# Last stage of a four-stage image kernel: planes and pixels fetched from SBUF to SBUF, and the first tile's features made among the channel maxima

## The reference

```
patches = unfold(x, 3x3, stride 2, padding 1)      # (B, C, 3, 3, 128, 128)
x1 = patches.max(axis=1)    # maxima over the 32 channels, 9 rows
x2 = patches.max(axis=2)    # maxima over the rows of a patch, 96 rows
x3 = patches.max(axis=3)    # maxima over the columns of a patch, 96 rows
y  = relu(batchnorm(conv_w @ concat(x1, x2, x3)))  # 32*9*4 rows
out = mean over the 9 taps of patches * y          # 32*2*2 rows, laid back to 256 x 256
```

## Time and profile before

| | |
|---|---|
| runs | 3294.06 us median of 3 (3288.66 to 3294.98) |
| profiled execution | 3293.31 us, span 3291.5 us |
| PE matmul busy | 2702.1 us (82%) |
| DVE busy | 2660.9 us (81%) |
| ACT busy | 1813.8 us (55%) |
| POOL busy | 1831.8 us (56%) |
| DMA moved | 419.22 MB |
| mean granted TensorE clock | 0.935 |

### The profile page before, as it was taken

How to read it: one execution, slowest core, us unless ns; L and a number is a source line. 1 busy time by engine, 2 the same in 40 slices (tenths; PEclk the granted TensorE clock), 3 DMA queues, 4 the chain that set the end, 5 groups by cost and what they waited for, 6 DMA issues and landing times. The chain is left out here.

```text
span 3291.5 us, 45789 instructions
## 1 busy us (share of the span) xinstructions
PE 2702.1 (82%) x12733; PEld 2092.2 (64%) x12733; DVE 2660.9 (81%) x3579; ACT 1813.8 (55%) x2343; POOL 1831.8 (56%) x1296
## 2 busy tenths in 40 slices
PE   0086698899989579799999569889998957979998
PEld 0035577677757458577774468667775745857776
DVE  8985887788885898688888598878888499868887
ACT  7743655566543455565655265566564345555654
POOL 2013173599950436199990317269995044629998
PEclk9998899999999789899999879999999978989999
DMA  6732001988860200688880200289885020068984
GB/s 254 251 91 77 1 0 38 231 220 222 193 174 1 77 1 0 169 222 218 209 228 32 77 0 0 56 230 225 218 192 158 1 77 0 0 183 218 227 208 114
DMA packets 116200, 419.22 MB, mean 127 GB/s; under 512 B 16565, under 2 KB 30693, under 8 KB 105354
## 3 DMA queue, kind: packets, MB, share of 16 engines
q1 hardware_dynamic: 96058, 374.65, 44.1%
q10 hardware_dynamic: 18432, 38.54, 3.3%
q0 software_dynamic: 1616, 4.90, 0.5%
HBM read 340.57 MB, written 75.26 MB: 126 GB/s over the span
## 5 line engine op out<-in xcount | busy, mean ns | idle before, releaser
L895 POOL TENSOR_TENSOR work<-work 128x512 f32<-128x512 f32 x960 | 1283.3, 1342 | 415.4 <-DVE work L1307 314.8
L549 PE MATMUL psum<-workr,w 128*128 128x512 f32 (+1 forms) x5760 | 1366.9, 397 | 67.2 <-ACT workr L765 50.6
L549 PEld LDWEIGHTS psum<-workr,w 128*128 128x128 f32 (+1 forms) x5760 | 1086.5, 189 | 346.9 <-issue 51.4
L1298 DVE SCALAR_TENSOR_TENSOR work<-psum,work 128x512 f32<-128x512 f32 x1152 | 738.1, 679 | 34.9 <-POOL work L895 21.4
L518 PE MATMUL psum<-workr 128*128 128x512 f32 x2304 | 553.7, 403 | 21.5 <-DVE workr L1195 21.5
L869 POOL TENSOR_TENSOR work<-img 128x520 f32 (+1 forms) x256 | 387.2, 1544 | 284.7 <-DVE workr L1167 255.7
L518 PEld LDWEIGHTS psum<-workr 128*128 128x128 f32 x2304 | 441.6, 192 | 135.0 <-issue 24.7
L859 POOL TENSOR_TENSOR work<-work 128x1024 f32<-128x1024 f32 x40 | 114.1, 2886 | 485.2 <-DVE work L1081 483.0
L745 ACT CAST workr<-psum 128x650 fp32r<-128x650 f32 x128 | 90.0, 703 | 419.4 <-DVE psum L1274 411.8
L420 PE MATMUL psum<-work,taps 128*128 x1152 | 261.6, 391 | 44.4 <-DVE work L1039 44.4
L1271 DVE TENSOR_TENSOR psum<-psum,work 128x650 f32<-128x650 f32 x128 | 107.9, 843 | 210.0 <-ACT psum L738 209.7
(11 more groups left out here) (188 smaller groups left out, 3582.6 us busy)
## 6 DMA issues: line engine op xcount, KB each, us to landing
work<-gn_dram SPq DMA_DIRECT2D x256, 585.0 KB, 10.7
work<-gn_dram SPq DMA_DIRECT2D x256, 146.2 KB, 3.8
work<-gn_dram SPq DMA_DIRECT2D x128, 292.5 KB, 4.8
work<-in_x SPq DMA_DIRECT2D x16, 2048.0 KB, 7.2
img<-in_x SPq DMA_DIRECT2D x32, 1024.0 KB, 11.4
work<-in_mixw SPq DMA_DIRECT2D x64, 512.0 KB, 4.9
out_x<-work ACTq DMA_DIRECT2D x120, 256.0 KB, 6.4
gn_dram<-img SPq DMA_DIRECT2D x24, 1040.0 KB, 16.9
```

Of the source, the lines that this page charges most:

```text
L549: mm = T.matmul(bank(m % 6), w5[wt][0:kr, P * n:P * n + P], ft[0:kr], start=(i == 0), stop=(i == 4))
L895: G.tensor_tensor(acc_t[v], acc_t[v], pd_t[(9 * v + n) % 6], ALU.add).then_inc(s_acc, 1)
L1298: V.scalar_tensor_tensor(out=tile4(pd_t[m % 6]), in0=tile4(psum[:, m % 6, :]), scalar=0.0, in1=rv[:, q, y0:y0 + RT, x0:x0 + WO], op0=ALU.m ...
```

## The change

gn_dram and its stores are gone. load_planes and load_pixels read img itself. load_pixels does it with 16 transfers per pair, one for each quadrant and copy, where there were four. The waits on a stored chunk become waits on s_gn3, the normalised chunk. At the end of an image SP waits until all planes and pixels have landed before it goes on to the next image's rows.

The features of tile 0 are moved: ACT makes them (prepare(0)) right after the eight normalisations and before it copies the maxima; DVE's three steps for it stand behind reductions 20, 21 and 24, whose loop is written out. The features of tile 1 (prepare(1)) and the first two restores come after the stores to mx_dram. mxq moves from bank 0 to bank 5, and PE waits for the maxima's copies before the sixth output, which takes that bank.

```diff
+FIRST = (20, 21, 24)
...
-        mxq = psum[:, 0, :].rearrange("p (m2 m1 w) -> p m1 m2 w", m2=2, m1=2)
+        mxq = psum[:, 5, :].rearrange("p (m2 m1 w) -> p m1 m2 w", m2=2, m1=2)
...
-                    sp.dma_start(a_t[k][0:32, :], gn_dram[0:32, n9]).then_inc(s_ab3[k], 16)
+                    sp.dma_start(a_t[k][0:32, :], img[0:32, n9]).then_inc(s_ab3[k], 16)
...
                 def load_pixels(u8, k):
-                    for n in range(4):
-                        sp.dma_start(r_t[k][32 * n:32 * n + 32, :].rearrange("p (q n) -> p q n", q=4),
-                                     byq[:, :, ds(u8 * PW, 9 * PW)]).then_inc(s_inr[k], 16)
-
-                def store_rows(e):
-
-                    hold(sp, s_gn3, b * NCH + (e + 1))
-                    r0 = 0 if e == 0 else 1 + CR * e
-                    r1 = HO + 2 if e == NCH - 1 else 1 + CR * (e + 1)
-                    sp.dma_start(gn_dram[:, r0 * PW:r1 * PW], img[:, r0 * PW:r1 * PW]).then_inc(s_gnd[e], 16)
+                    for q in range(4):
+                        for n in range(4):
+                            sp.dma_start(r_t[k][32 * n:32 * n + 32, 9 * PW * q:9 * PW * (q + 1)],
+                                         img[32 * q:32 * q + 32, ds(u8 * PW, 9 * PW)]).then_inc(s_inr[k], 16)
...
                     if i < NPAIR - 2:
                         if i % 2 == 0:
-                            hold(sp, s_gnd[i // 2 + 1], b * 16 + 16)
+                            hold(sp, s_gn3, b * NCH + (i // 2 + 2))
...
-                store_rows(0)
-                hold(sp, s_gnd[0], b * 16 + 16)
+                hold(sp, s_gn3, b * NCH + 1)
                 load_planes(0, 0)
                 load_pixels(0, 0)
                 load_planes(RP, 1)
-                store_rows(1)
-                store_rows(2)
                 hold(sp, s_ones, b * 2 + 2)
                 hold(sp, s_mxd, b * 32 + 32)
                 load_maxima(sp, 0, 0)
                 for i in range(NPAIR - 1):
                     load_next(i)
-                    if i % 2 == 1 and i // 2 + 3 < NCH:
-                        store_rows(i // 2 + 3)
+                for p in range(2):
+                    hold(sp, s_ab3[p], b * (96 * (NPAIR // 2)) + 96 * (NPAIR // 2))
+                    hold(sp, s_inr[p], b * (256 * (NPAIR // 2)) + 256 * (NPAIR // 2))
...
                 for n in range(6):
+                    if n == 5:
+                        pe.wait_ge(s_mxz, b * 4 + 4)
+                        pe.wait_ge(s_mxl, b * 2 + 2)
                     product(n, n, terms, range(4))
...
+                def prepare(k):
+
+                    shifted(0, 0, k)
+                    high(0, 0, k, free=False)
+                    side_high(0, 0, k)
+                    side_low(0, 0, k)
+
+                act.wait_ge(s_tail, b * 32 + 16)
+                act.wait_ge(s_guard, b * 3 + 3)
+                prepare(0)
                 act.wait_ge(s_mxp, b * (NT + 1) + (NT + 1))
...
-                act.wait_ge(s_tail, b * 32 + 16)
-                act.wait_ge(s_guard, b * 3 + 3)
+                prepare(1)
                 for k in range(2):
-                    shifted(0, 0, k)
-                    high(0, 0, k, free=False)
-                    side_high(0, 0, k)
                     restore(0, k)
-                    side_low(0, 0, k)
...
-                with v.Fori(0, NT // 4) as j:
-                    for k in range(4):
-                        v.wait_ge(s_mxp, b * (NT + 1) + j * 4 + (k + 1))
-                        V.tensor_reduce(mx_rq[:, ds(j * (4 * RT) + k * RT, RT), :],
-                                        psum[:, 2 + k, :].rearrange("p (r q c) -> p r q c", r=RT, q=4), AX.X, ALU.max
-                                        ).then_inc(s_mxr, 1)
+                for n in range(NT):
+                    v.wait_ge(s_mxp, b * (NT + 1) + (n + 1))
+                    V.tensor_reduce(mx_rq[:, RT * n:RT * n + RT, :],
+                                    psum[:, 2 + n % 4, :].rearrange("p (r q c) -> p r q c", r=RT, q=4), AX.X, ALU.max
+                                    ).then_inc(s_mxr, 1)
+                    if n in FIRST:
+                        front(0, 0, 0, FIRST.index(n))
...
-                    v.wait_ge(s_inr[p], b * (32 * NPAIR) + j * 64 + 64)
+                    v.wait_ge(s_inr[p], b * (128 * NPAIR) + j * 256 + 256)
...
-                for k in range(2):
-                    for step in range(3):
-                        front(0, 0, k, step)
+                for step in range(3):
+                    front(0, 0, 1, step)
                 pair(0, 0, first=True)
```

More of the change, by code:

```diff
@@ L107, in build @@
         SMALL_BANK = 6
-        gn_dram = nc.dram_tensor("gn_dram", (P, IMG_N), F32, kind="Internal").ap()
         bn_dram = nc.dram_tensor("bn_dram", (2, 9 * P), F32, kind="Internal").ap()
@@ L248, in build @@
         s_gn3 = sem("s_gn3")
-        s_gnd = [sem(f"s_gnd{e}") for e in range(NCH)]
         s_mxp, s_mxr, s_mxz, s_mxd = sem("s_mxp"), sem("s_mxr"), sem("s_mxz"), sem("s_mxd")
@@ L331, in _ @@
                     sp.dma_start(wr[k], mixw[:, 1024 * (8 + k):1024 * (9 + k)]).then_inc(s_w[k], 16)
-                byq = gn_dram.rearrange("(q c) n -> c q n", q=4)
                 def load_planes(u8, k):
                     n9 = ds(u8 * PW, 9 * PW)
-                    sp.dma_start(a_t[k][0:32, :], gn_dram[0:32, n9]).then_inc(s_ab3[k], 16)
[L338 to L342, removed]
@@ new lines, in load_planes @@
+                    sp.dma_start(b_t[k][0:32, PW:10 * PW], img[32:64, n9]).then_inc(s_ab3[k], 16)
+                    sp.dma_start(a_t[k][64:128, :], img[0:64, n9]).then_inc(s_ab3[k], 16)
+                    sp.dma_start(a_t[k][32:64, :], img[64:96, n9]).then_inc(s_ab3[k], 16)
+                    sp.dma_start(b_t[k][32:64, PW:10 * PW], img[96:128, n9]).then_inc(s_ab3[k], 16)
+                    sp.dma_start(b_t[k][64:128, PW:10 * PW], img[64:128, n9]).then_inc(s_ab3[k], 16)
+                def load_pixels(u8, k):
+                    for q in range(4):
+                        for n in range(4):
+                            sp.dma_start(r_t[k][32 * n:32 * n + 32, 9 * PW * q:9 * PW * (q + 1)],
+                                         img[32 * q:32 * q + 32, ds(u8 * PW, 9 * PW)]).then_inc(s_inr[k], 16)
@@ L532, in _ @@
                 for q in range(4):
-                    mm = T.transpose(bank(0)[:, P * q:P * q + P], mxt[:, P * q:P * q + P], cs("ident"))
+                    mm = T.transpose(bank(5)[:, P * q:P * q + P], mxt[:, P * q:P * q + P], cs("ident"))
                 mm.then_inc(s_mxp, 1)
@@ L720, in _ @@
                                  ).then_inc(s_gn3, 1)
[L721 to L727, removed]
-                act.wait_ge(s_guard, b * 3 + 3)
-                act.dma_start(mx_dram[0:HO, MXI:MXR], mz.bitcast(F32)).then_inc(s_mxd, 16)
-                act.dma_start(mx_dram[1:HO + 1, 0:MXI], mz[:, MXI:2 * MXI].bitcast(F32)).then_inc(s_mxd, 16)
                 def shifted(j, p, k):
@@ L782, in _ @@
                     side_high(0, 0, k)
+                    side_low(0, 0, k)
+                act.wait_ge(s_tail, b * 32 + 16)
+                act.wait_ge(s_guard, b * 3 + 3)
+                prepare(0)
+                act.wait_ge(s_mxp, b * (NT + 1) + (NT + 1))
+                for v in (0, 2):
+                    A.copy(mzq[:, v, :, 1:3, :], mxq).then_inc(s_mxz, 1)
+                    A.copy(mzq[:, v, :, 0, 1:WO], mxq[:, :, 1, 0:WO - 1]).then_inc(s_mxz, 1)
+                act.wait_ge(s_mxz, b * 4 + 4)
+                act.wait_ge(s_mxl, b * 2 + 2)
+                act.wait_ge(s_guard, b * 3 + 3)
+                act.dma_start(mx_dram[0:HO, MXI:MXR], mz.bitcast(F32)).then_inc(s_mxd, 16)
+                act.dma_start(mx_dram[1:HO + 1, 0:MXI], mz[:, MXI:2 * MXI].bitcast(F32)).then_inc(s_mxd, 16)
+                prepare(1)
+                for k in range(2):
                     restore(0, k)
-                    side_low(0, 0, k)
                 def step(j, p, more=True):
```

## The result

The changed kernel takes 3265.91 us (median of 4 runs, 3264.38 to 3268.44) against 3291.36 for the one before; the ratio is 0.9923, 95% interval 0.9908 to 0.9937: 25 us faster. The direction was as forecast, the size was not: 15 us were predicted, and the range ended at 3269. The forecast started from 3294.06, the median of three runs; a fourth (3288.46) moved the median of the kernel before to 3291.36, so 2.7 of the 13 us between 3279 and 3265.91 belong to the base. The profiled execution has a span of 3263.9 us, 27.6 less.

A forecast was written before the change was run, and what follows sets the result against it. The prediction took PE to set the last stage's pace and ACT's features to bound its start. It took 3.8 us off each of four images, 15.1 in all, from 3294.06 to 3279.0 us; range 3269 to 3292.

The forecast's parts named there:

- The start before is bound by ACT's features: Start of the last stage: PE idles 12.64 us until ACT completes the first tile's features, not until the maxima land.
- Features among the maxima cost 2.9 us there and nothing on ACT: Tile 0's features lengthen DVE's chain of reductions by 2.9 us (2.5 to 3.3); ACT's work ends before the maxima arrive.
- Then the maxima's round trip is the bound, and it is short because the row stores are gone: Start of the last stage: PE waits for load_maxima; stores land in 5.6 us, not 12.0, the load in 3.0.
- Sum for one image, taken on PE's stream: Last stage's start: an all-warm product stream as if begun at 2929.7 instead of 2933.5, 3.8 us gained per image.
- Its pace is PE's: Last stage: PE's matmuls set the pace, 180 in 42.60 us per two pairs of tiles, plus a gap of 0.62.
- 43.2 us per two pairs unchanged: Steady part of the last stage: the time per two pairs would stay; the prediction is wrong if it moved.
- the forecast's own 4.5 to 5.5: Start of the last stage: DVE's first product expected 4.5 to 5.5 us earlier.
- the cold start: PE's first matmuls after idling run at a lowered clock; 1.6 us charged per image, before and after the change.
- The transfers from SBUF cost nothing: Planes and pixels read from img: put at nothing; sixteen issues cost SP 8 us a pair, the bytes 11 us.
- The new holds: End of an image: SP waits for the last pixels before fetching rows; nothing charged, 2 us an image if uncovered.
- (a): Start of the last stage: the maxima's round trip isn't shorter and becomes the bound; +10 us, 3304; chance 0.09.
- (e): More gain: no DVE wait, load_maxima in 2.5 us, no clock fall; 6.3 us an image, 3269; chance 0.08.

The follow-up runs named there:

- fetch_only: The kernel before with only the transfers, waits and holds of the change, the order of ACT, DVE and PE as before: 3292.2 us, ratio 0.9998.
- order_only: The change with gn_dram, its stores and its four pixel transfers put back, tile 0's features still among the maxima: 3280.96 us, ratio 0.9966 to the kernel before.
- four_terms: The change with the third of the five matmuls of each output left out: 3264.3 us, ratio 0.9912 to the kernel before.
- late_store: The change with the store of a pair's second tile moved behind the next pair's shifted copies on ACT: 3252.05 us, ratio 0.9875 to the kernel before.
- half_adds: The change with each of POOL's adds on 256 of the 512 columns: 3223.8 us, ratio 0.9788 to the kernel before.
- warm: The change with 20 further, unused matmuls on PE while it waits for the maxima: 3265.15 us, ratio 0.9915 to the kernel before.
- split32: The change with each pixel transfer cut in two, 32 per pair for the same bytes: 3552.8 us, ratio 1.0793 to the kernel before.

## Why the prediction was too small

*The start before is bound by ACT's features.* Right, shown by fetch_only.

*Features among the maxima cost 2.9 us there and nothing on ACT.* Right: the stores went out at +29.88 where +27.08 had been, 2.8 us; ACT was done with its side copies at 584.4, 2.9 us before the maxima came.

*Then the maxima's round trip is the bound, and it is short because the row stores are gone.* Right, shown by fetch_only (5.3 us without them, against 12.0 before) and by order_only (9.0 to 9.3 with them, against 5.2 to 5.3 in the change). The sizes were a little high: stores 0.3 us too late, 3.0 us taken for the load's landing where it was 2.4 to PE's start. PE went on at +38.0, not +39.0, and at +38.5 in the third image. That is 3.6 us in all.

*Sum for one image, taken on PE's stream.* This is the step that failed, by the sentence "Its pace is PE's". 42.60 us of work in 43.22 looked like it, but the 0.62 us were the sign that PE waits for somebody. The pace was set by the loop DVE's sum, POOL, ACT's store, ACT's shifted copies and DVE's maxima: four_terms (PE's work down by a fifth, the stage by 0.4%), late_store and half_adds show it. The sign that the prediction named, 43.2 us per two pairs unchanged, did come true (43.22, from 735.09 to 778.31), but it comes true with either pace and couldn't tell them apart. What counts is then when the first product comes, and that was 5.8 us earlier, as the forecast's own 4.5 to 5.5 nearly said; the cold start and PE's place in its stream are taken up by its gaps (warm). This is 1.0 us an image, 4.0 in all: what is left of the 22.7 us of the four stages after the forecast's 15.1 and the 3.6 above.

*What lies outside the last stage* was put at nothing, without a reason. It gave 4.8 us. The rows show a clock that rises earlier after the start of both convolutions, and their shorter times fit it. Before and fetch_only, whose images take the same time, agree there (391.8 us each time), and the other kernels lie between 388.1 and 392.4, four_terms with 392.4 even above. Why a given kernel gets the earlier rise wasn't tried, and the cause stays open. As far as the prediction goes, these 4.8 us are luck. 15.1 + 3.6 + 4.0 + 4.8 = 27.5, against 27.6 measured in span.

*The transfers from SBUF cost nothing.* Right for the time: the steady pairs are unchanged, and the DMA share over 600 to 900 us fell from 0.89 to 0.82. The price of their issue was wrong: 16 take SP 11.3 us or more, not 8, and with the planes some 17 of 21.6 us are filled. The 8 us were taken from transfers that read DRAM. The advice to coalesce many small transfers (the Trainium skill, "DMA: Bandwidth & Descriptors", "Rules for kernel authors") begins to matter here between 16 and 32 transfers a pair: split32 shows it, with transfers of 83 and 66 KB, and the price is SP's issue time of 0.67 to 0.69 us each, not the 2 us each that the prediction took from the same page of the Trainium skill. There the Trainium skill gives that cost for one transfer; that twelve more would add up in series was the prediction's own step, and 22 transfers a pair that land in 2.4 to 5.2 us each and still fit into 21.6 us show that they don't.

*The new holds* cost nothing: fetch_only has them and is at 0.9998.

Of the rivals, (a) named the right bound; its price was avoided because the row stores were what filled the queues, as fetch_only shows without them and order_only with them. (e) came nearest in size, for other reasons.

## What to carry to other kernels

An engine at 99% with small, regular gaps is not yet the one that sets the pace: look at what ends the gaps, follow it until the loop closes, and price a shift of the start at the loop's first instruction, not at the busiest engine's stream. The share of busy time can hide waiting inside the spans; leaving out part of an engine's work tells more. Two edits that bring 0 and 1.7 us a stage alone can bring 5.7 together, when one removes the first bound and the other the second. Before a small urgent load is issued, look what is already in the queues: here it was worth more to send the large store behind it than to make the store ahead of it smaller.

## What was not expected of the hardware

A transfer of 32 partitions from SBUF kept SP longer than the same one from DRAM: 592 ns against 422 for the second plane transfer of each pair (medians of 13 and 14), at about equal landing times (2.6 and 2.8 us). Instruction rows from 600 to 900 us, the change, then the kernel before:

```profile
L336 SPq DMA_DIRECT2D work<-img x13: 592/592/602, 616.7 to 877.1; - x13
```

```profile
L338 SPq DMA_DIRECT2D work<-gn_dram x14: 411/422/423, 601.0 to 882.8; - x14
```

With nearly the same idle time before it (10.12 and 10.16 us) and the same work, PE ran the first 6.0 us of the next image's convolution at 1.2 GHz before the change and the first 3.3 after it, and the first 6.2 and 3.2 of the third stage. The stages between two last stages took 388.1 to 392.4 us over all kernels here; this clock is a part of that, and in the Fourier stage something else moved up to 1.7 us.
